# Cross attention in a two-attention kernel: wider weight loads for the transposes of P, and the projections moved between their two halves

## The chip, the cores and the metric

The kernel runs on one core of a Trainium2 chip. The metric is the device time of one execution in microseconds (us), as the median of several runs. Engines are named as in the profile: PE is TensorE's matmul, PEld its weight load, DVE VectorE, ACT ScalarE, POOL GpSimd, SP SyncE.

## The reference, cut to what matters

A batch of 32 sequences of 128 tokens, width 128, goes through a cross attention, a mixture of experts, a second cross attention (16 heads of width 8 over 77 context tokens) and two layers of local attention with a feed-forward part. The change touches only the second cross attention:

```python
def _L1_xattn_ref(q, k, v, mask, w_q, w_k, w_v, w_o):
    ...
    query = proj(q, w_q)
    key_ = proj(k, w_k)
    value = proj(v, w_v)
    scores = jnp.einsum('bhqd,bhkd->bhqk', query, key_) / jnp.sqrt(jnp.asarray(D_K, dtype=query.dtype))
    scores = jnp.where(mask == 0, jnp.asarray(NEG, dtype=scores.dtype), scores)
    attn = jax.nn.softmax(scores, axis=-1)
    out = jnp.einsum('bhqk,bhkd->bhqd', attn, value)
    out = out.transpose(0, 2, 1, 3).reshape(B, -1, H * D_K)
    return out @ w_o.T
...
x = x + _L1_xattn_ref(_layernorm(x, axis=-1), ctx_1024, ctx_1024, mask_1x1xSxS2_ik0, L1_xattn_w_q, L1_xattn_w_k, L1_xattn_w_v, L1_xattn_w_o)
```

## The kernel before, in words

The stages follow one another: first attention (tiles `a_...`), routing and experts (`r_...`, `b_...`), second cross attention (`c_...`), local attention (`d_...`) and feed-forward (`f_...`). The second cross attention is a software pipeline over the 32 sequences. Each engine runs its own program, written out by hand (`c_tensor`, `c_scalar`, `c_vector`, `c_pool`), once per step; `it.b(5)` is the sequence that is five steps old, and semaphores are all that ties the engines. In one step, in this order:

- PE: the transposes of the probabilities P of the older sequence, heads 0 to 7 (L1311, eight transposes of `c_p` into `slot1`; I call them PTa), then mask and scores of the next sequence, heads 0 to 7 (L1321, L1326; Sa), then heads 8 to 15 of both (PTb, Sb, the same lines), then the three projections of a yet younger sequence (L1337 values, L1338 queries, L1339 keys), then P times V (L1353), the transpose of the normalised input (L1360) and the output projection (L1364).
- ACT: copies PTa out of PSUM (L1378 `c_pT`), exponentials of heads 0 to 7 (L728, eight activations), copies PTb out, copies the projections out (L1387 to L1391), exponentials of heads 8 to 15.
- DVE: reciprocal of the sums of heads 8 to 15 (L1415 `c_rc`), layer norm, the largest score of each head after Sa and after Sb (L1407 `c_nm`), the mix of the experts' answers into X (L1436) and its statistics (L1440 to L1445), reciprocal of heads 0 to 7 (L1415), splitting of the projections into high and low parts (L1452 to L1461), copies and the sum into X (L1473 to L1478).
- POOL: normalises P of heads 8 to 15 (L1510 `c_p`), gathers expert answers (L1523, L1527), a reciprocal root (L1031 `rs`), the copy of a context (L1539 `c_c`), normalises P of heads 0 to 7 (L1510).

Every engine works its list off in order. PTa waits for the last of POOL's entries in the step before it, and PTb for the first of its own step. Both halves of the transposes use the two banks of `slot1`, so PTb also waits until ACT has copied PTa out. `c_p` holds, for each of 128 tokens, 16 rows of 77 probabilities, one head behind the other. In a few of the steps large copies for a later stage (`wqkv`, `w1l`) stand behind the step's own work on ACT and DVE.

Of the kernel before, what the change touches and what calls it, by code (L numbers as in the profile page):

```python
# [16 lines left out]
NB = 32  # L17
T = 128
D = 128
SK = 77  # L20
# [82 lines left out]
def nth(n, j, k):  # L103

    return (n - 1) * k + j


def count(b, j=1, k=1, base=0):

    return (b + base) * k + j  # L110


def program(nc, out, x_in, ctx_in, mask_in, wq0_in, wkv0_in, wo0_in, nrm0_in, wg_in, w1e_in, w3e_in, w2e_in,
            l1_in, wqkv_in, qks_in, wol_in, lng_in, w1l_in, b1l_in, w2l_in,
            ident_in, band_in, rot_in, keyi_in, head_in):
    with ExitStack() as ctx:
        def sem(name):
            return ctx.enter_context(nc.semaphore(name))
# [5 lines left out]
        def at(name, shape, dt=F32):  # L124
            size = 2 if dt == BF16 else 4
            for n in shape[1:]:
                size *= n
            t = nc.alloc_sbuf_tensor_at(name, shape, dt, offset=room[0])
            room[0] += (size + 31) // 32 * 32
            assert room[0] <= nc.sbuf_usable_end, name  # L130
            return t


        R = [ctx.enter_context(nc.psum_tensor(f"slot{i}", [128, 2, 512], F32)) for i in range(4)]
# [10 lines left out]
        ident = at("ident", [128, 128])  # L145
# [81 lines left out]
        l1 = at("l1", [128, 4, 128])  # L227
# [106 lines left out]
        def S(name):  # L334
            if name not in made:
                made[name] = sem(name)
            return made[name]
# [950 lines left out]
        def c_tensor(e):  # L1288
            t = c_

            def body(it):
                if it.static and it.i == 2:
                    e.wait_ge(S("b_xl"), LAST + 1)
                    e.wait_ge(S("c_const"), 1)
                if it.static and it.i == 4:
                    e.wait_ge(S("b_gT"), LAST + 1)
                    e.wait_ge(S("b_ye"), LAST + 1)
                if it.static and it.i == 5:
                    e.wait_ge(S("b_g"), LAST + 1)
                for half, slot in ((0, 2), (1, 3)):  # L1300
                    b = it.b(5)
                    if b is not None:
                        if half == 0:
                            if it.seen(6):
                                e.wait_ge(S("ac_pTb"), it.upto(6, NB))
                        else:
                            if it.seen(5):
                                e.wait_ge(S("ac_pTa"), it.upto(5, NB))
                        e.wait_ge(S("c_pn"), count(b, half + 1, 2))
                        for k in range(8):  # L1310
                            mm = e.transpose(R[1][0:SK, k // 4, 128 * (k % 4):128 * (k % 4) + 128],  # L1311
                                             t["p"][:, it.m(5, 2), 8 * half + k, :], ident[:])
                        mm.then_inc(S(("ac_PTa", "ac_PTb")[half]), 1)
                    b = it.b(4)
                    if b is not None:
                        e.wait_ge(S("c_sp"), count(b, 1, 3))
                        e.wait_ge(S("c_sp"), count(b, 3, 3))
                        if it.seen(5):
                            e.wait_ge(S("c_rc"), nth(it.upto(5), half + 1, 2))
                        for k in range(2):  # L1320
                            e.matmul(R[slot][:, k, 0:4 * SK], identb[:], maskb[:].rearrange("p a b -> p (a b)"),  # L1321
                                     start=True, stop=False)
                        for n, (w, x) in enumerate(((1, 0), (0, 1), (0, 0))):
                            for k in range(2):
                                o = 32 * (2 * half + k)
                                mm = e.matmul(R[slot][:, k, 0:4 * SK], t["qT"][w][o:o + 32, it.m(4, 2), :],  # L1326
                                              t["kb"][x][o:o + 32, it.m(4, 2), :, :].rearrange("p a b -> p (a b)"),
                                              start=False, stop=(n == 2))
                        mm.then_inc(S(("ac_Sa", "ac_Sb")[half]), 1)
                b = it.b(3)  # L1330
                if b is not None:
                    if it.seen(4):
                        e.wait_ge(S("c_sp"), nth(it.upto(4), 3, 3))
                    e.wait_ge(S("ac_xh"), count(b, base=NB))
                    e.wait_ge(S("ac_ch"), count(b, base=NB))
                    c = t["c"][:, it.m(3, 4), :]
                    e.matmul(R[0][0:SK, 0, 256:384], c, l1[:, 2, :], start=True, stop=True)  # L1337
                    e.matmul(R[0][:, 0, 0:128], l1[:, 0, :], t["xT"][:, it.m(3, 2), :], start=True, stop=True)  # L1338
                    e.matmul(R[0][:, 0, 128:128 + SK], l1[:, 1, :], c, start=True, stop=True).then_inc(S("c_proj"), 1)  # L1339
                if it.b(5) is not None or it.b(2) is not None or it.b(6) is not None:  # L1340
                    if it.seen(6):
                        e.wait_ge(S("ac_oTe"), it.upto(6, NB))
                    if it.seen(3):
                        e.wait_ge(S("ac_xh"), it.upto(3, NB))
                    if it.seen(7):
                        e.wait_ge(S("ac_add"), it.upto(7, NB))
                b = it.b(5)
                if b is not None:
                    e.wait_ge(S("ac_pTb"), count(b, base=NB))
                    for j in range(4):  # L1350
                        for g in range(4):

                            mm = e.matmul(R[0][32 * g:32 * g + 32, 1, 0:128],  # L1353
                                          t["vz"][0:SK, it.m(5, 4), g, 32 * j:32 * j + 32], t["pT"][0:SK, 4 * g + j, :],
                                          start=(j == 0), stop=(j == 3))
                    mm.then_inc(S("ac_PV"), 1)
                b = it.b(2)
                if b is not None:
                    e.wait_ge(S("ac_xn"), count(b, base=NB))
                    e.transpose(R[0][:, 1, 128:256], t["xn"][:, it.m(2, 2), :], ident[:]).then_inc(S("ac_xTp"), 1)  # L1360
                b = it.b(6)
                if b is not None:
                    e.wait_ge(S("ac_oTe"), count(b, base=NB))
                    e.matmul(R[0][:, 1, 256:384], t["oT"][:, it.m(6, 2), :], l1[:, 3, :], start=True, stop=True)\  # L1364
                        .then_inc(S("ac_wo"), 1)
            return body
# [786 lines left out]
```

## Time and profile before

| what | value |
|---|---|
| median of 3 runs | 1761.24 us (1760.27 to 1763.22) |
| the profiled execution | 1751.36 us |
| its span in the trace | 1749.4 us |
| busy: PE, PEld, DVE, ACT, POOL | 89%, 72%, 69%, 66%, 57% |
| the c stage, first transposes of P to the last | 624.1 to 992.0 us |

The profiled execution is 9.9 us shorter than the median, and 2.0 us of it lie outside the span. The page cuts the span into 40 slices of 43.7 us; the c stage lies in slices 15 to 23 counted from one. Busy shares are averages over stages with different limits, so the c stage has to be read by itself.

### The profile page before, as it was taken

Reading aid. Unit: us, or ns where it says so; the run is one execution under the profiler, and the core shown is the slowest. Engines: PE = TensorE matmul, PEld = TensorE weight load, DVE = VectorE, ACT = ScalarE, POOL = GpSimd, SP = SyncE. Lnnn points to the kernel's source line nnn. Section 1 sums busy time; section 2 is a strip of 40 time slices with the busy share of each in tenths; the row PEclk is TensorE's granted clock in tenths of the full one; section 3 lists DMA queues with packets and bytes.
Section 4 is the critical chain, followed back from the end, with each engine's and each line's share of the span. In section 5 each row is a group of like instructions: output and inputs, shape, how many; then the busy total and the mean of one; then the engine's idle time right before and its main releaser. Section 6 shows DMA issues by size and latency. Waiting matters only on the chain.

```text
span 1749.4 us, 37345 instructions
## 1 busy us (share of the span) xinstructions
PE 1555.5 (89%) x11418; PEld 1268.3 (72%) x11419; DVE 1210.9 (69%) x3059; ACT 1155.1 (66%) x3175; POOL 988.7 (57%) x853
## 2 busy tenths in 40 slices
PE   5899999899889879897877689999979799999988
PEld 3677777677667756665656478888868588888766
DVE  6888888888665554545555378888846677777656
ACT  5888788687555565666566467887753487777732
POOL 5668877688430055555554277777720577777500
PEclk8999999999999965557577699999999999999999
DMA  9700000000123210000000000000000000000000
GB/s 385 268 1 10 10 12 9 10 16 11 43 74 84 75 51 12 27 13 12 9 12 6 6 12 16 14 15 15 14 9 7 5 14 15 15 15 15 10 18 36
DMA packets 75555, 61.29 MB, mean 35 GB/s; under 512 B 40256, under 2 KB 61120, under 8 KB 74688
## 3 DMA queue, kind: packets, MB, share of 16 engines
q1 hardware_dynamic: 71360, 51.69, 9.2%
q0 software_dynamic: 4096, 8.40, 1.6%
q8 instruction: 47, 0.77, 0.2%
q14 instruction: 52, 0.43, 0.1%
HBM read 21.30 MB, written 30.41 MB: 30 GB/s over the span
## 4 chain that ended last, share of the span: by engine, by line
PE 57%; DVE 23%; ACT 6%; POOL 6%; issue 6%; DMA 1%; DVEq 0%; POOLq 0%; SPq 0%; ACTq 0%
PE slot L1311 6%; PE slot L1647 6%; PE slot L453 5%; PE slot L455 4%; PE slot L454 4%; PE slot L1630 4%; PE slot L1591 4%; PE slot L1326 3%; PE slot L1600 3%; ACT a_p L728 3%; PE slot L1665 3%; DVE a_sum L846 3%; POOL a_rq L1092 2%; PE slot L1881 2%; POOL c_p L1510 2%
## 5 line engine op out<-in xcount | busy, mean ns | idle before, releaser
L1031 POOL TENSOR_TENSOR rs<-mv,nhalf 128x1 f32 (+1 forms) x160 | 93.5, 584 | 276.9 <-DVE mv L1445 155.3
L1797 POOL TENSOR_TENSOR d_A<-d_A,d_B 128x1024 f32<-128x1024 f32 x64 | 150.7, 2355 | 130.2 <-DVE d_B L1743 130.2
L1801 POOL TENSOR_TENSOR d_r<-d_vv,nhalf 128x16 f32<-128x16 f32 x64 | 186.5, 2914 | 47.6 <-DVE d_vv L1765 47.1
L728 ACT ACTIVATE d_p<-slot,d_nm,d_r 128x128 f32<-128x128 f32 x512 | 186.0, 469 | 25.7 <-DVE d_nm L1756 25.7
L728 ACT ACTIVATE a_p<-slot,a_nm,a_rq 128x77 f32<-128x77 f32 x512 | 163.9, 433 | 54.8 <-DVE a_nm L754 54.8
L728 ACT ACTIVATE c_p<-slot,c_nm 128x77 f32<-128x77 f32 x512 | 143.8, 379 | 43.0 <-DVE c_nm L1407 43.0
L1311 PE MATMUL slot<-ident,c_p 128*77 128x128 f32 x512 | 113.0, 391 | 52.0 <-POOL c_p L1510 50.7
L1407 DVE TENSOR_REDUCE c_nm<-slot 128x8 f32<-128x616 f32 x64 | 51.1, 799 | 143.7 <-PE slot L1326 143.7
L1311 PEld LDWEIGHTS slot<-ident,c_p 128*77 128x77 f32 x512 | 92.0, 222 | 69.6 <-POOL c_p L1510 45.9
L1647 PE MATMUL slot<-d_v,d_pT 128*128 128x65 f32 x1024 | 121.8, 272 | 1.4 <-ACT d_pT L1684 1.4
L1378 ACT ACTIVATE c_pT<-slot 77x1024 f32<-77x1024 f32 x64 | 68.5, 1070 | 80.7 <-PE slot L1311 80.5
L1647 PEld LDWEIGHTS slot<-d_v,d_pT 128*128 128x128 f32 x1024 | 119.4, 192 | 2.1 <-ACT d_pT L1684 1.8
L736 POOL TENSOR_TENSOR a_p<-a_p,a_rc 128x616 f32<-128x616 f32 x64 | 80.1, 1251 | 72.1 <-DVE a_rc L848 71.7
L728 ACT ACTIVATION_READ_ACCUMULATOR c_p<-slot,c_nm 128x1 f32 x512 | 116.0, 230 | 0.0
L1724 DVE TENSOR_TENSOR d_A<-slot,T 128x1024 f32<-128x1024 f32 x64 | 78.3, 1224 | 44.4 <-PE slot L1591 42.9
L1752 DVE TENSOR_REDUCE slot<-slot 128x8 f32<-128x1024 f32 x64 | 78.9, 1233 | 31.4 <-PE slot L1630 28.6
L1092 POOL TENSOR_TENSOR a_rq<-a_vvq,nhalf 128x16 f32<-128x16 f32 x32 | 95.0, 2969 | 1.8 <-DVE a_vvq L961 1.8
L1695 ACT ACTIVATE d_oT<-slot 128x512 f32<-128x512 f32 x64 | 38.2, 597 | 78.3 <-PE slot L1641 78.3
L1510 POOL TENSOR_TENSOR c_p<-c_p,c_rc 128x616 f32<-128x616 f32 x64 | 78.8, 1232 | 18.4 <-DVE c_rc L1415 18.4
L607 PE MATMUL slot<-a_kb,a_qT 128*128 128x154 f32 x512 | 81.3, 303 | 8.4 <-DVE a_pT L889 7.3
L1527 POOL DMA_INDIRECT c_yg<-answers,c_gi x64 | 63.6, 994 | 36.7 <-POOL c_gi L1523 26.3
L1047 POOL DMA_INDIRECT routed<-r_xn,r_ps x64 | 65.0, 1016 | 34.1 <-issue 21.7
(282 smaller groups left out, 4738.9 us busy)
## 6 DMA issues: line engine op xcount, KB each, us to landing
routed<-zero SPq DMA_DIRECT2D x2, 9216.0 KB, 49.3
b_x<-routed SPq DMA_DIRECT2D x80, 64.0 KB, 1.8
answers<-b_y SPq DMA_DIRECT2D x40, 128.0 KB, 1.9
X<-in_x SPq DMA_DIRECT2D x2, 1024.0 KB, 7.3
d_zx<-Z SPq DMA_DIRECT2D x64, 32.0 KB
H<-Z SPq DMA_DIRECT2D x64, 32.0 KB
out<-f_o SPq DMA_DIRECT2D x8, 256.0 KB, 2.0
d_zx<-Z SPq DMA_DIRECT2D x64, 31.8 KB
```

The costliest lines, as they stand in the source:

```text
L453: e.matmul(o, ws[1], xs[0], start=True, stop=False)
L607: mm = e.matmul(R[slot][:, k // 2, 2 * SK * (k % 2):2 * SK * (k % 2) + 2 * SK], a["qT"][:, c, :], a["kb"][:, it.m(2, 2), c // 2, :], start ...
L728: i = e.activation(t["p"][:, h, :], R[slot][:, k // nbank, nk * (k % nbank):nk * (k % nbank) + nk], ACT.Exp, bias=t["nm"][:, h:h + 1], sca ...
L736: return e.tensor_tensor(p, p, t["rc"][:, h].unsqueeze(2).to_broadcast([128, h.stop - h.start, nk]), ALU.mult)
L1031: return e.tensor_tensor(rs[:, bass.ds(b, 1)], mv[:, bass.ds(b, 1), 1:2].rearrange("p a b -> p (a b)"), nhalf[:, 0:1], ALU.pow)
L1092: e.tensor_tensor(a["rq"][:, it.m(1, 2), :], a["vvq"][:], nhalf[:, 0:16], ALU.pow).then_inc(S("a_rq"), 1)
L1311: mm = e.transpose(R[1][0:SK, k // 4, 128 * (k % 4):128 * (k % 4) + 128], t["p"][:, it.m(5, 2), 8 * half + k, :], ident[:])
L1510: e.tensor_tensor(p, p, c_["rc"][:, h].unsqueeze(2).to_broadcast([128, 8, SK]), ALU.mult)\
L1647: mm = e.matmul(R[3][:, h // 4, 65 * (h % 4):65 * (h % 4) + 65], t["pT"][:, 4 * (h % 2) + h // 2, :], t["v1"][:, it.m(5, 4), h, :], start= ...
L1752: e.tensor_reduce(R[1][:, 0, 0:8], R[2][:].rearrange("p a (j k) -> p a j k", k=128), AX.X, ALU.max, negate=True)\
L1797: e.tensor_tensor(t["A"][:, p, :], t["A"][:, p, :], t["B"][:, p, :], ALU.add).then_inc(S("d_key"), 1)
L1801: e.tensor_tensor(t["r"][:, it.m(2, 4), :], t["vv"][:, p, :], nhalf[:, 0:16], ALU.pow).then_inc(S("d_key"), 1)
```

## The change

The transposes of P take their weights from `flat`, in which the eight heads of a half lie behind one another. Each now loads 128 columns instead of 77, from the start of its head, except the last of a half, which loads 77. Rows 77 to 127 of the transposed result hold columns of the next head, and no instruction reads them: the copy by ACT (L1378) and P times V take rows 0 to 76, as before. The block of the three projections moves from behind Sb to between Sa and PTb, with its waits. The other engines' programs are as they were.

```diff
                         e.wait_ge(S("c_pn"), count(b, half + 1, 2))
+                        flat = t["p"][:, it.m(5, 2), 8 * half:8 * half + 8, :].rearrange("p h k -> p (h k)")
                         for k in range(8):
-                            mm = e.transpose(R[1][0:SK, k // 4, 128 * (k % 4):128 * (k % 4) + 128],
-                                             t["p"][:, it.m(5, 2), 8 * half + k, :], ident[:])
+                            w = min(128, (8 - k) * SK)
+                            mm = e.transpose(R[1][0:w, k // 4, 128 * (k % 4):128 * (k % 4) + 128],
+                                             flat[:, SK * k:SK * k + w], ident[:])
                         mm.then_inc(S(("ac_PTa", "ac_PTb")[half]), 1)
...
                         mm.then_inc(S(("ac_Sa", "ac_Sb")[half]), 1)
-                b = it.b(3)
-                if b is not None:
-                    if it.seen(4):
-                        e.wait_ge(S("c_sp"), nth(it.upto(4), 3, 3))
-                    e.wait_ge(S("ac_xh"), count(b, base=NB))
-                    e.wait_ge(S("ac_ch"), count(b, base=NB))
-                    c = t["c"][:, it.m(3, 4), :]
-                    e.matmul(R[0][0:SK, 0, 256:384], c, l1[:, 2, :], start=True, stop=True)
-                    e.matmul(R[0][:, 0, 0:128], l1[:, 0, :], t["xT"][:, it.m(3, 2), :], start=True, stop=True)
-                    e.matmul(R[0][:, 0, 128:128 + SK], l1[:, 1, :], c, start=True, stop=True).then_inc(S("c_proj"), 1)
+                    if half == 0:
+                        b = it.b(3)
+                        if b is not None:
+                            if it.seen(4):
+                                e.wait_ge(S("c_sp"), nth(it.upto(4), 3, 3))
+                            e.wait_ge(S("ac_xh"), count(b, base=NB))
+                            e.wait_ge(S("ac_ch"), count(b, base=NB))
+                            c = t["c"][:, it.m(3, 4), :]
+                            e.matmul(R[0][0:SK, 0, 256:384], c, l1[:, 2, :], start=True, stop=True)
+                            e.matmul(R[0][:, 0, 0:128], l1[:, 0, :], t["xT"][:, it.m(3, 2), :], start=True, stop=True)
+                            e.matmul(R[0][:, 0, 128:128 + SK], l1[:, 1, :], c, start=True, stop=True).then_inc(S("c_proj"), 1)
```

On PE, one step of the c stage stands like this before the change; the names are tiles of the program, output before inputs, and the sizes are those of the output.

```order
L1311 MATMUL slot<-ident,c_p 77x128 x8
L1321 MATMUL slot<-maskb,identb 128x308 x2
L1326 MATMUL slot<-c_kbh,c_qTl 128x308 x2
L1326 MATMUL slot<-c_kbl,c_qTh 128x308 x2
L1326 MATMUL slot<-c_kbh,c_qTh 128x308 x2
L1337 MATMUL slot<-l_127,c_c 77x128
L1338 MATMUL slot<-c_xT,l_127 128x128
L1339 MATMUL slot<-c_c,l_127 128x77
L1353 MATMUL slot<-c_pT,c_vz 32x128 x16
```

These rows begin with PTb: the projections follow Sb and P times V follows them. After the change the same engine has, from PTa of a step on:

```order
L1313 MATMUL slot<-ident,c_p 128x128 x7
L1313 MATMUL slot<-ident,c_p 77x128
L1323 MATMUL slot<-maskb,identb 128x308 x2
L1328 MATMUL slot<-c_kbh,c_qTl 128x308 x2
L1328 MATMUL slot<-c_kbl,c_qTh 128x308 x2
L1328 MATMUL slot<-c_kbh,c_qTh 128x308 x2
L1340 MATMUL slot<-l_127,c_c 77x128
L1341 MATMUL slot<-c_xT,l_127 128x128
L1342 MATMUL slot<-c_c,l_127 128x77
L1313 MATMUL slot<-ident,c_p 128x128 x7
L1313 MATMUL slot<-ident,c_p 77x128
```

Seven of the eight transposes of a half write 128 rows instead of 77, and the three projections stand ahead of PTb and Sb instead of behind Sb. No instruction is added or removed.

## Rows read from the trace of the kernel before

**Rows 1.** The page: busy by engine, PE's granted clock in 40 slices.

```profile
span 1749.4 us, 37345 instructions
PE 1555.5 (89%) x11418; PEld 1268.3 (72%) x11419; DVE 1210.9 (69%) x3059; ACT 1155.1 (66%) x3175; POOL 988.7 (57%) x853
PEclk8999999999999965557577699999999999999999
```

**Rows 2.** Stretches: length, busy by engine, granted clock, DMA share, GB/s.

```profile
611.00:996.00 385.00, 312.74 (x2341) 238.16 (x2342) 189.95 (x633) 228.60 (x1191) 189.11 (x244) 0.63 0.06 17
648.20:736.90 88.70, 81.49 (x529) 61.89 (x527) 42.78 (x142) 52.25 (x274) 46.48 (x60) 0.50 0.07 20
736.90:743.70 6.80, 4.13 (x57) 3.24 (x57) 4.83 (x19) 4.23 (x27) 2.89 (x5) 1.00 0.04 10
```

**Rows 3.** Timeline of PE over one step at the lower clock, and the step's neighbours.

```profile
669.61 1.99 PE L1311 MATMUL slot<-ident,c_p 128*77 128x128 f32 x8 [0.92 <-POOL c_p L1510]
...
673.11 1.99 PE L1311 MATMUL slot<-ident,c_p 128*77 128x128 f32 x8
...
676.61 0.71 PE L1337 MATMUL slot<-l,c_c 128*77 128x128 f32 x2
...
678.01 1.94 PE L1353 MATMUL slot<-c_pT,c_vz 77*32 77x128 f32 x32
...
681.70 0.71 PE L1311 MATMUL slot<-ident,c_p 128*77 128x128 f32 x2 [0.92 <-POOL c_p L1510]
```

**Rows 4.** The chain that ended last, in the same step.

```profile
676.72 0.80 DVE c_nm L1407
677.52 0.27 DVE X L1436
678.98 0.17 DVE mv L1445
679.99 0.48 POOL c_c L1539
680.46 1.19 POOL c_p L1510
681.70 1.35 PE slot L1311 x5
```

**Rows 5.** Timeline of POOL: both normalisations of P, and the gather between.

```profile
671.27 1.21 POOL L1510 TENSOR_TENSOR c_p<-c_p,c_rc 128x616 f32<-128x616 f32 x1
674.77 0.96 POOL L1527 DMA_INDIRECT c_yg<-answers,c_gi  x1 [0.31 <-issue]
```

**Rows 6.** Timeline of PE: first transposes of the stage, and PTa thirty steps on.

```profile
624.12 1.96 PE L1311 MATMUL slot<-ident,c_p 128*77 128x128 f32 x8 [3.36 <-POOL c_p L1510]
970.04 1.91 PE L1311 MATMUL slot<-ident,c_p 128*77 128x128 f32 x8
```

**Rows 7.** Timeline of PE in steps with some full clock.

```profile
734.27 1.99 PE L1311 MATMUL slot<-ident,c_p 128*77 128x128 f32 x8
736.05 0.72 PE L1321 MATMUL slot<-maskb,identb 128*128 128x308 bf16 x2
790.13 1.10 PE L1311 MATMUL slot<-ident,c_p 128*77 128x128 f32 x8 [2.46 <-POOL c_p L1510]
792.45 1.99 PE L1311 MATMUL slot<-ident,c_p 128*77 128x128 f32 x8
795.51 0.44 PE L1337 MATMUL slot<-l,c_c 128*77 128x128 f32 x2
796.01 0.34 PE L1339 MATMUL slot<-c_c,l 128*128 128x77 f32 x2
```

**Rows 8.** Timeline of PE in the d stage: transposes with 128-column weights.

```profile
1277.81 1.91 PE L1600 MATMUL slot<-ident,d_p 128*128 128x128 f32 x8
1279.51 0.64 PE L1627 MATMUL slot<-bandb,identb 128*128 128x512 bf16 x2
```

**Rows 9.** Timeline of PE: a step with a large copy on DVE.

```profile
710.08 1.99 PE L1311 MATMUL slot<-ident,c_p 128*77 128x128 f32 x8 [0.65 <-POOL c_p L1510]
```

## The prediction

> **What bounds the kernel now.** I read the page first. PE is busy 89% of the span, and its granted clock is near full everywhere but in the c stage, where the slices fall to 5 to 7 tenths [rows 1]. The table of stretches gives the mean over 611 to 996 us as 0.63 [rows 2]. The clock has two levels, 0.50 (1.2 GHz) and 1.00 (2.4 GHz): 648.2 to 736.9 is all at 0.50, then comes a stretch of 6.8 us at 1.00, 736.9 to 743.7 [rows 2]. So full clock held in (0.63 - 0.50) / 0.50 = 26% of 385 us, about 100 us, or some 15 stretches of 6.8 us.
>
> Then I read one step at the lower clock. PTa starts at 669.61 and the next one at 681.70: 12.09 us [rows 3]. PE runs without a gap from PTa through Sa, PTb and Sb until the projections start at 676.61. The chain of waits leaves PE there: DVE takes the largest scores at 676.72, mixes X at 677.52, finishes the statistics at 678.98, POOL copies the context at 679.99 and normalises P of heads 0 to 7 from 680.46, and PTa follows [rows 4]. This is a loop of two parts:
> - the **PE part**, from PTa to the reduction after Sb, 676.72 - 669.61 = 7.1 us at the lower clock;
> - the **DVE and POOL part**, 681.70 - 676.72 = 5.0 us, which TensorE's clock does not touch.
>
> The projections, P times V, the input's transpose and the output projection run beside the second part. PE still idles 0.92 us there [rows 3]. The mean step over thirty steps is (970.04 - 624.12) / 30 = 11.53 us [rows 6], so the full stretches give back, net of the steps disturbed by large copies, 0.56 us a step.
>
> **The move of the projections.** They start at 676.61 and P times V at 678.01, which makes 1.40 us at the lower clock [rows 3]. At full clock they begin at 795.51 and the last begins at 796.01 and takes 0.34, so 0.84 us at most [rows 7]. Today DVE and POOL cover them. After the change they stand between Sa and PTb, inside the PE part, and queued behind them are PTb and Sb. DVE waits for Sb, and its mix, POOL's root, context copy and normalisation wait for DVE. Is there slack before PTb that could absorb them? At the lower clock, no: PTb starts at 673.11 without an idle mark, while POOL's normalisation of heads 8 to 15 ended at 671.27 + 1.21 = 672.48 [rows 3, 5]. So PE alone set it, and 1.40 us go onto the loop. The other end of the bound: with PTa at full clock, PTb starts 2.32 us after it [rows 7], against a normalisation that ends 672.48 - 669.61 = 2.87 us after PTa in the step at the lower clock [rows 3, 5]; if it ended as late in that step, up to half a microsecond could be absorbed. In the steps with a large copy there is slack too, 0.65 us [rows 9], in about three steps. The gather on POOL ends at 675.73 [rows 5], 3 us ahead of its next use, and is no bound. The sequences have projections ahead of PTb or Sb in 31 steps: 31 x 1.40 = **+43 us**. Off that go 3 x 0.65 = **-2 us**. What the move takes off PE's list behind Sb is worth nothing, since PE was not late there; it turns 0.92 us of idle into 2.3.
>
> **The wider loads.** Seven transposes of eight load 128 columns instead of 77. The first of eight 77-column transposes starts at 734.27 and the instruction behind them at 736.05: 1.78 us at the lower clock [rows 7]. Eight 128-column transposes in the d stage, also at the lower clock by the same division, take 1279.51 - 1277.81 = 1.70 us [rows 8]. The load width does not set the pace, and I cost the edit at **0**. The load lies beside the previous transpose; uncovered, it could cost at most a few hundredths of a microsecond per transpose. The Trainium skill speaks against this ("TensorE: Matmul & The Clock Gate", section LDWEIGHTS): a load takes its number of columns at 1.2 GHz, so 51 more columns would be some 43 ns, and if none of it were covered, 14 x 32 x 43 ns = 19 us, an estimate by that page. The two rows disagree with it as a cost on the path.
>
> **The clock.** This is the open term. PE work at full clock takes 1.10 us where it takes 1.99 at the lower one, or 0.44 against 0.71: a factor of 1.6 to 1.8, and I take 1.75 [rows 3, 7]. One full stretch of 6.8 us that spans the 5.0 us of DVE and POOL leaves 1.8 us for the PE part, which saves 1.8 x 0.75 = 1.35 us. The rise at 736.9 came just behind a burst of eight transposes, 734.27 to 736.05, in an unbroken run of PE since PTa [rows 7]. The step at 669.61 has the same run and no rise [rows 3], so the run as it is now is just enough in some steps and not in others. After the change the unbroken run is 8.5 instead of 7.1 us, and projections join directly onto a burst. I expect more stretches, 23 instead of 15 over thirty-odd steps: 8 x 1.35 = **-11 us**. In some five steps the projections themselves then run at full clock, saving 1.40 - 0.84 = 0.56 each: **-3 us**. The bounds: no rise at all would lose today's gift, 31 x 0.56 = 17 us, and full clock throughout the PE part would save far more (below). I take a value near the present state, since the content of the run hardly changes.
>
> The Trainium skill says of transposes on the same page (Part 4: PE-mode transpose) that they do not count as PE-busy in the way matmuls do. By that, only the moved projections would matter. The rise right behind eight transposes does not look like it.
>
> **Sum.** 43 - 2 - 11 - 3 = +27 us. On the profiled 1751.4 us this is 1778; the median is 9.9 us above the profiled execution, so 1761.2 + 27 = **1788 us**.
>
> **The rivals.**
> - *The clock pays for the move.* The longer run raises the clock early in nearly every step. At full clock the PE part would be about 8.5 / 1.75 = 4.9 us. Today's mean PE part is 11.53 - 5.0 = 6.5 us. The change gains once the new one is below that, when (8.5 - 6.5) / (8.5 - 4.9) = 56% of it runs at full clock. If a rise comes about 3 us into each step, the PE part is 3 + 5.5 / 1.75 = 6.1 us, and 31 x 0.4 less the 2 of the large copies makes -14 us: 1747. Full clock throughout would give 31 x 1.6 = -50 us: 1711. For it: today's run is at the edge of raising the clock. Against: in the stretch from 736.9 to 743.7, over DVE's and POOL's part, PE was busy for only 4.13 of 6.8 us, and then the clock fell [rows 2]; the change makes this idle time longer. Chance 0.28, of which 0.07 for far below 1740.
> - *The two cancel.* Rises in every step, but late in it: within 0.2%. Chance 0.07.
> - *Fewer rises.* PE's idle time of 0.92 us before PTa grows to 2.3, the busy share falls, and the clock stays low: 43 - 2 + 17 = +58, 1819 us. For it: the stage's clock is already the lowest of the kernel. Against: rises follow dense runs, and those get longer. Chance 0.08.
> - *Wider loads cost.* If the load sets the pace in part, some 10 to 19 us more: 1803. The d stage's rows speak against. Chance 0.05.
>
> **How the numbers follow.** The forecast has 0.52; its own range is 1776 to 1802: with no more stretches than today the sum is 43 - 2 - 0 - 0 = +41, with thirty it is 43 - 2 - 20 - 6 = +15. Slower than 0.2% (about what a measurement here can tell): 0.52 + 0.08 + 0.05 = 0.65; same 0.07; faster 0.28. The range for 8 in 10 takes in the first rival's moderate form and leaves out full clock throughout and most of the case without rises: 1742 to 1808.
>
> **What the changed profile would show.** At the lower clock PTa to PTb is 4.9 us instead of 3.5, and PTa to the reduction 8.5 instead of 7.1, with 5.0 behind it unchanged. Eight transposes take 1.8 us at the lower clock as before. PE's idle mark before PTa grows to about 2.3 us. The granted clock over the stage is 0.65 to 0.72. The a, b, d and f stages keep their times. I am wrong if the stage's clock is above 0.75, if the part behind the reduction is not 5.0 us, or if the eight transposes take over 2.0.

## The result and the profile after

The changed kernel takes 1806.92 us (median of 4 runs, 1800.59 to 1810.39), against 1760.76 us for the kernel before in the same comparison: ratio 1.026, 95% interval 1.0239 to 1.0281. It is 46 us slower. The forecast was 1788 us, 27 us slower, with a range of 1742 to 1808: the direction and the place were right, the size was short by 19 us. The result lies 1 us inside that range and above the 1776 to 1802 of the forecast's own mechanism.

The profiled execution took 1800.59 us. Of the page, the busy shares and PE's granted clock in 40 slices:

```profile
span 1798.6 us, 37345 instructions
PE 1565.9 (87%) x11418; PEld 1278.0 (71%) x11419; DVE 1216.0 (68%) x3059; ACT 1160.5 (65%) x3175; POOL 989.3 (55%) x853
PEclk9999999999989856655655679999999999999999
```

Against [rows 1] PE is busy 10.4 us more, DVE and ACT some 5 us, POOL 0.6 us, while the span grew by 49.2 us: most of the added time is waiting. The stretches of the c stage (length, busy by engine, granted clock, DMA share, GB/s):

```profile
631.00:985.00 354.00, 276.39 (x1969) 214.48 (x1969) 160.35 (x541) 195.13 (x1003) 166.28 (x214) 0.57 0.05 13
676.80:683.60 6.80, 3.33 (x51) 2.46 (x51) 4.84 (x19) 4.15 (x24) 2.20 (x4) 1.00 0.04 10
690.50:693.80 3.30, 1.62 (x37) 1.18 (x35) 2.75 (x10) 2.38 (x17) 0.39 (x1) 1.00 0.00 0
693.90:741.60 47.70, 38.97 (x248) 30.55 (x249) 21.44 (x72) 25.38 (x126) 25.05 (x32) 0.50 0.09 25
```

Over these 27 steps the clock is 0.57, so it is full for 14% of them; before it was 0.63 and 26% over the whole stage [rows 2]. In the full stretch from 676.80 PE is busy for 3.33 of 6.8 us; in the one of before in [rows 2] it was 4.13. For a fair comparison, the first 28 steps from PTa to PTa, of the kernel before and then of the changed one:

```profile
624.12:950.50 326.38, 275.29 (x2043) 210.00 (x2043) 167.58 (x561) 197.98 (x1040) 170.23 (x219) 0.62 0.05 14
631.02:998.37 367.35, 287.30 (x2043) 222.91 (x2043) 166.10 (x561) 202.22 (x1040) 170.29 (x219) 0.57 0.05 12
```

They take 41 us more. Over the first thirty steps (624.12 to 970.04 us before, 631.02 to 1016.85 us after) the trace of before has 13 stretches of full clock, 88 us in all; the changed one has 12, but seven of them are only half as long, and they make 63 us.

One step at the lower clock, timeline of PE:

```profile
695.66 1.97 PE L1313 MATMUL slot<-ident,c_p 128*128 128x128 f32 x8 [3.53 <-POOL c_p L1513]
697.42 0.72 PE L1323 MATMUL slot<-maskb,identb 128*128 128x308 bf16 x2
...
699.14 0.71 PE L1340 MATMUL slot<-l,c_c 128*77 128x128 f32 x2
...
700.41 1.91 PE L1313 MATMUL slot<-ident,c_p 128*128 128x128 f32 x8
...
703.83 1.94 PE L1356 MATMUL slot<-c_pT,c_vz 77*32 77x128 f32 x32
...
708.92 0.69 PE L1313 MATMUL slot<-ident,c_p 128*128 128x128 f32 x2 [2.32 <-POOL c_p L1513]
```

It answers to [rows 3]. From PTa to the end of Sb, where the next block begins, it is 703.83 - 695.66 = 8.17 us; before it was 676.61 - 669.61 = 7.00. The step is 708.92 - 695.66 = 13.26 instead of 12.09 us. Both differences are 1.17 us. PE's idle mark before PTa went from 0.92 to 2.32. The eight transposes take 697.42 - 695.66 = 1.76 us, as they did with 77 columns.

Over thirty steps, and where the stage begins (timeline of PE):

```profile
617.63 0.68 PE L1340 MATMUL slot<-l,c_c 128*77 128x128 f32 x2 [1.31 <-POOL c_c L1542]
631.02 0.45 PE L1313 MATMUL slot<-ident,c_p 128*128 128x128 f32 x1 [4.58 <-POOL c_p L1513]
1016.85 0.85 PE L1313 MATMUL slot<-ident,c_p 128*128 128x128 f32 x6 [0.68 <-POOL c_p L1513]
```

The mean step is (1016.85 - 631.02) / 30 = 12.86 us, against 11.53 [rows 6]: 30 x 1.33 = 40 us. Of this, 1.17 a step is the longer step at the lower clock. The other 0.16 is a balance (13.26 - 12.86 = 0.40 us a step by which the mean is shorter, formerly 0.56): the full stretches give back less, and the steps with large copies cost less than before. The first projections of the stage start 5.8 us later than in the trace of before:

```profile
611.83 0.47 PE L1337 MATMUL slot<-l,c_c 128*77 128x128 f32 x1 [1.70 <-POOL c_c L1539]
```

That difference arose before any changed instruction, so it belongs to the two executions that were profiled, not to the change. 40 + 5.8 leaves 3 us: 1.17 for the one block of projections that runs ahead of an Sb before the first PTa, and 2 for the stage's end.

### The profile page after: what moved, and what is told of

It reads as the page before. It is cut to its first block, busy times and chain, and to the rows that moved or that the text cites. A ratio compares the mean times of both kernels' runs of the same rounds, so it can differ in the third digit from the quotient of the medians.

```text
span 1798.6 us, 37345 instructions
## 1 busy us (share of the span) xinstructions
PE 1565.9 (87%) x11418; PEld 1278.0 (71%) x11419; DVE 1216.0 (68%) x3059; ACT 1160.5 (65%) x3175; POOL 989.3 (55%) x853
## 4 chain that ended last, share of the span: by engine, by line
PE 58%; DVE 22%; POOL 6%; ACT 6%; issue 6%; DMA 1%; DVEq 0%; POOLq 0%; SPq 0%; ACTq 0%
PE slot L1313 6%; PE slot L1650 5%; PE slot L453 5%; PE slot L455 4%; PE slot L454 4%; PE slot L1633 4%; PE slot L1328 4%; PE slot L1594 4%; PE slot L1603 3%; ACT a_p L728 3%; PE slot L1668 3%; DVE a_sum L846 2%; POOL a_rq L1092 2%; PE slot L1884 2%; POOL c_p L1513 2%
## 5 line engine op out<-in xcount | busy, mean ns | idle before, releaser
L1313 PE MATMUL slot<-ident,c_p 128*128 128x128 f32 (+1 forms) x512 | 116.8, 403 | 88.9 <-POOL c_p L1513 87.8
L1313 PEld LDWEIGHTS slot<-ident,c_p 128*128 128x128 f32 (+1 forms) x512 | 100.5, 222 | 97.4 <-POOL c_p L1513 73.6
```

The costliest lines, as they stand in the source:

```text
L1313: mm = e.transpose(R[1][0:w, k // 4, 128 * (k % 4):128 * (k % 4) + 128], flat[:, SK * k:SK * k + w], ident[:])
```

## The experiments

Two theories of the change stood at first. **A**: the projections lie on the loop's PE part, the width of the loads is free, and most of the price comes from the lower clock. **B**: the width has a share, by its pace or by the clock. A second question came from the forecast's open term: what makes the clock fall in this stage, and what does it cost? The letters in an expectation are its own and go on from there. Ratios are against the kernel before, run beside each.

### e1: the wide loads alone

```diff
+                        flat = t["p"][:, it.m(5, 2), 8 * half:8 * half + 8, :].rearrange("p h k -> p (h k)")
                         for k in range(8):
+                            w = min(128, (8 - k) * SK)
-                            mm = e.transpose(R[1][0:SK, k // 4, 128 * (k % 4):128 * (k % 4) + 128],
-                                             t["p"][:, it.m(5, 2), 8 * half + k, :], ident[:])
+                            mm = e.transpose(R[1][0:w, k // 4, 128 * (k % 4):128 * (k % 4) + 128],
+                                             flat[:, SK * k:SK * k + w], ident[:])
```

> The kernel before with the 128-column loads alone. Theory A (the width is free and leaves the clock as it is): within 4 us of before, eight transposes 1.7 to 1.8 us at the lower clock, granted clock over the c stage 0.62 to 0.64. Rival B (wider loads keep the clock up): clock above 0.66 and 10 us or more faster. Rival C (wider loads cost): 10 to 19 us slower.

Measured: 1753.95 us, ratio 1.0004 (0.9993 to 1.0016). The stage in its trace, and one burst of transposes:

```profile
611.00:996.00 385.00, 318.98 (x2338) 242.69 (x2339) 189.13 (x632) 227.98 (x1189) 187.56 (x241) 0.61 0.06 16
```

```profile
672.30 1.97 PE L1313 MATMUL slot<-ident,c_p 128*128 128x128 f32 x8
674.06 0.72 PE L1323 MATMUL slot<-maskb,identb 128*128 128x308 bf16 x2
```

Eight wide transposes take 1.76 us and the clock is 0.61, just under what A named. The width does nothing that can be measured, either to the pace or to the clock. Rivals B and C fall, and with them the theory that the width has a share.

### e2: the move alone

The diff of the change without the lines of e1.

> The kernel before with the projections between Sa and PTb alone, loads of 77 columns. Theory A: PTa to the reduction after Sb is 8.3 us instead of 7.1 at the lower clock, the part behind it stays 5.0, and the time is that of the full change, 1800 to 1812. Rival: the full change owes part of its 46 us to the width, and this one lies at 1790 or below, or at 1820 or above.

Measured: 1796.87 us, ratio 1.0247 (1.0227 to 1.0268), which covers the change's 1.026. The time lies below A's 1800 and above the rival's 1790, because the kernel before took 1753.54 us beside this run and not 1760.76; the ratio decides. A step at the lower clock:

```profile
716.73 1.99 PE L1311 MATMUL slot<-ident,c_p 128*77 128x128 f32 x8 [2.31 <-POOL c_p L1511]
...
720.23 0.71 PE L1338 MATMUL slot<-l,c_c 128*77 128x128 f32 x2
...
721.50 1.91 PE L1311 MATMUL slot<-ident,c_p 128*77 128x128 f32 x8
...
724.92 1.94 PE L1354 MATMUL slot<-c_pT,c_vz 77*32 77x128 f32 x32
```

724.92 - 716.73 = 8.19 us, as in the change. Within these intervals the move is the whole effect.

### e3 and e4: idle transposes at the end of each step

```diff
                         .then_inc(S("ac_wo"), 1)
+                if it.b(5) is not None and it.b(0) is not None:
+                    for j in range(8):
+                        e.transpose(R[1][:, j // 4 % 2, 128 * (j % 4):128 * (j % 4) + 128], ident[:], ident[:])
```

They write slot1 after ACT has read it and before PTa overwrites it, and nobody reads the result. PE does more work, none of it useful. It stands in the first 27 of the 32 steps that have transposes of P. e4 has 16.

> The kernel before with eight transposes of the identity into slot1, which nobody reads, behind the output projection of each step of the c stage up to the 32nd. Theory D (the clock falls because PE's work thins out between Sb and the next PTa): the granted clock over the stage rises above 0.8 and the time falls by 20 to 60 us, to 1700 to 1740. Rival E (the clock does not follow this): eight transposes at the lower clock take 1.7 us against 0.9 us of idle time, so each step is 0.8 us longer and the time 1785.

> The same with sixteen. Theory D: clock at 0.95 or more over the stage, steps of 9.3 to 9.8 us, time 1695 to 1715, since sixteen transposes at full clock take 1.75 us against 2.3 us of idle time. Rival E: 2.5 us more per step, time near 1835.

Measured: e3 1706.12 us, ratio 0.9733 (0.9712 to 0.9755); e4 1709.27 us, ratio 0.9755 (0.9735 to 0.9775). Of e3's trace, the first 28 steps and one step of PE at full clock:

```profile
624.30:903.00 278.70, 220.00 (x2258) 177.17 (x2258) 166.36 (x560) 195.50 (x1040) 169.05 (x219) 0.91 0.06 16
```

```profile
672.94 1.10 PE L1311 MATMUL slot<-ident,c_p 128*77 128x128 f32 x8 [0.73 <-POOL c_p L1513]
...
675.25 1.10 PE L1311 MATMUL slot<-ident,c_p 128*77 128x128 f32 x8 [0.33 <-POOL c_p L1513]
...
677.17 0.44 PE L1337 MATMUL slot<-l,c_c 128*77 128x128 f32 x2
...
680.54 1.04 PE L1368 MATMUL slot<-ident 128*128 128x128 f32 x8
682.24 0.99 PE L1311 MATMUL slot<-ident,c_p 128*77 128x128 f32 x7 [0.66 <-POOL c_p L1513]
```

The granted clock is 0.91, against 0.62 over the same 28 steps before, and the step is 682.24 - 672.94 = 9.30 us instead of 12.09. PTa to the projections is 4.23 us instead of 7.00, and the rest stays 5.07. So theory D's forecast came, and rival E falls: more PE work between the output projection and the next PTa raises the clock, and the lower clock costs up to 2.8 us a step. That it has to stand in this gap, and that thin work there is what lets the clock fall, these two runs do not show.

Twice the filler brings nothing more in time, though it raises the clock over the same stretch from 0.91 to 0.95, as expected:

```profile
624.00:903.00 279.00, 232.72 (x2484) 191.95 (x2482) 167.35 (x565) 196.37 (x1041) 169.68 (x220) 0.95 0.06 16
```

The Trainium skill ("TensorE: Matmul & The Clock Gate", Part 4: PE-mode transpose) says that transposes do not count as PE-busy in the way matmuls do. Here filler made of nothing but transposes raised the granted clock from 0.62 to 0.91; the measurement decides against it.

### e5: the change with the same eight

> The changed kernel with the eight idle transposes at each step's end. Theory A (the move costs what stands on PE's part of the loop, and most of that price is the lower clock's): with the clock kept up the projections add 0.3 to 0.5 us a step, since PTb waits for POOL anyway until 2.3 us after PTa, so 1715 to 1725, against 1706 for the kernel before with the same filler. Rival F (the move costs the same 43 to 46 us whatever the clock): near 1750.

Measured: 1723.34 us, ratio 0.9814 (0.9787 to 0.9842). A step at full clock:

```profile
661.48 1.09 PE L1313 MATMUL slot<-ident,c_p 128*128 128x128 f32 x8 [2.53 <-POOL c_p L1516]
...
664.07 1.04 PE L1313 MATMUL slot<-ident,c_p 128*128 128x128 f32 x8
...
671.02 1.09 PE L1313 MATMUL slot<-ident,c_p 128*128 128x128 f32 x8 [0.88 <-POOL c_p L1516]
```

The step is 671.02 - 661.48 = 9.54, so the move costs 0.24 us here against 1.17 at the lower clock, and somewhat less than the 0.3 to 0.5 expected: PTb waits for POOL anyway in e3, idle mark 0.33, and the projections run in that time. The ratios of e5 and e3 differ by 0.0081, 14 us (8 to 20 by the two intervals), of which 31 x 0.24 = 7 is this. The clock over 27 steps is 0.88 instead of e3's 0.91:

```profile
623.40:906.00 282.60, 217.21 (x2185) 175.93 (x2186) 160.66 (x540) 189.41 (x1003) 166.76 (x214) 0.88 0.06 16
```

The other half is there in the first three steps, before the clock of e5 stays up (e5, then e3):

```profile
623.42 1.94 PE L1313 MATMUL slot<-ident,c_p 128*128 128x128 f32 x8 [4.59 <-POOL c_p L1516]
```

```profile
624.31 1.96 PE L1311 MATMUL slot<-ident,c_p 128*77 128x128 f32 x8 [3.37 <-POOL c_p L1513]
...
654.15 1.10 PE L1311 MATMUL slot<-ident,c_p 128*77 128x128 f32 x8 [0.62 <-POOL c_p L1513]
```

They take 661.48 - 623.42 = 38.06 us in e5 and 654.15 - 624.31 = 29.84 in e3, 8 us more. Rival F, 43 us at any clock, falls.

### e6: the projections between PTb and Sb

```diff
                         mm.then_inc(S(("ac_PTa", "ac_PTb")[half]), 1)
+                    if half == 1:
+                        ...
                     b = it.b(4)
```

The block of the projections stands there whole, and no longer behind Sb.

> The kernel before with the projections between PTb and Sb, loads of 77 columns. Theory A: they stand on the same part of the loop, so at the lower clock PTa to PTb is 3.5 and PTa to the reduction 8.2 to 8.5 us; time 40 to 50 us above before, as for the change. Rival G (the harm comes from tearing Sa and PTb apart, and with them ACT's copies): clearly less than 40.

Measured: 1792.28 us, ratio 1.0219 (1.0179 to 1.0259), 38 us slower, just under the 40 to 50 that A named; the interval, 31 to 45, holds the lower part of that. The step at the lower clock:

```profile
699.68 1.99 PE L1311 MATMUL slot<-ident,c_p 128*77 128x128 f32 x8 [3.52 <-POOL c_p L1511]
...
703.18 1.99 PE L1311 MATMUL slot<-ident,c_p 128*77 128x128 f32 x8
...
707.88 1.94 PE L1354 MATMUL slot<-c_pT,c_vz 77*32 77x128 f32 x32
```

PTa to PTb is back at 3.50, and PTa to the end of Sb is 8.20 all the same. Between these two places ahead of Sb it makes little difference. Rival G, that tearing Sa and PTb apart does the harm, has at most the few us by which 38 lies under e2's 43.

### e7: the projections at the head of the step

The same block ahead of the loop over the halves, before PTa's wait for POOL.

> The kernel before with the projections at the head of the step, ahead of PTa's wait for POOL. Theory A: they fill idle time there; the input's transpose is copied 0.4 us before PTa could start, so 1.0 us of 1.35 comes onto the loop at the lower clock, and PTa to the reduction stays 7.1. Time 1780 to 1790 if the clock stays at 0.63 over the stage; less if the shorter idle time raises it. Rival G: no cost, 1755.

Measured: 1745.16 us, ratio 0.993 (0.9907 to 0.9953): 12 us faster than before (8 to 16). Its first 28 steps, and a step whose clock is low at its start:

```profile
628.90:943.00 314.10, 241.65 (x2045) 191.70 (x2045) 167.87 (x564) 195.80 (x1040) 167.49 (x220) 0.72 0.05 14
```

```profile
785.83 1.84 PE L1321 MATMUL slot<-ident,c_p 128*77 128x128 f32 x8
787.51 0.43 PE L1331 MATMUL slot<-maskb,identb 128*128 128x308 bf16 x2
...
788.86 1.09 PE L1321 MATMUL slot<-ident,c_p 128*77 128x128 f32 x8 [0.30 <-ACT c_pT L1378]
...
792.79 1.08 PE L1353 MATMUL slot<-c_pT,c_vz 77*32 77x128 f32 x32 [1.96 <-ACT c_pT L1378]
...
794.96 0.71 PE L1307 MATMUL slot<-l,c_c 128*77 128x128 f32 x2 [0.60 <-DVE c_xT L1476]
...
796.23 1.91 PE L1321 MATMUL slot<-ident,c_p 128*77 128x128 f32 x8
```

Projections and PTa now form one burst, the clock rises behind PTa, and Sa, PTb and Sb run at 2.4 GHz. The step is 796.23 - 785.83 = 10.40 us. The clock is 0.72, against 0.62 over 28 steps before. The forecast of 1780 to 1790 was for an unchanged clock, and its price was too high besides. The next step is all at the lower clock:

```profile
796.23:808.65 12.42, 11.01 (x74) 8.57 (x74) 6.83 (x25) 6.85 (x37) 6.50 (x8) 0.50 0.04 12
```

It is 0.33 us longer than the 12.09 of before, not 1.0. At that price an unchanged clock would have given about 1766. The projections start behind DVE's copy of `c_xT`, as expected. In this step PE idles 12.42 - 11.01 = 1.41 us, more than the 0.92 of before; so the amount of idle time alone does not decide the level of the clock. Why this order raises it stays open.

### e8 and e9: how much filler, and e7 with filler

> The kernel before with twelve idle transposes. Theory D: between e3 and e4, which lie within 3 us of one another: 1700 to 1710, with fewer falls of the clock than eight and cheaper ones than sixteen.

Measured: 1708.43 us, ratio 0.9728 (0.9674 to 0.9781). The number between 8 and 16 makes no difference to the time that these runs can tell.

> The kernel of e7, projections at the head of the step, with the eight idle transposes at its end. Theory H (e7 gained through the clock alone, its position on the loop costs time): with the clock kept up by the filler nothing is left to gain, and the projections at full clock delay PTa by 0.2 to 0.4 us a step: 1710 to 1720, behind e3's 1706. Rival I (the position itself is better): below 1700.

Measured: 1737.27 us, ratio 0.9922 (0.9895 to 0.9949). Theory H's 1710 to 1720 and rival I's time below 1700 both missed: it is far behind e3, and no faster than e7 (0.993) beyond the intervals, although the filler raised the clock over the first 28 steps from 0.72 to 0.83. PE in one step:

```profile
789.82 0.31 PE L1336 MATMUL slot<-c_kbh,c_qTh 32*128 32x308 f32 x2
792.07 1.08 PE L1353 MATMUL slot<-c_pT,c_vz 77*32 77x128 f32 x32 [1.94 <-ACT c_pT L1381]
...
793.47 1.91 PE L1368 MATMUL slot<-ident 128*128 128x128 f32 x8
795.17 0.63 PE L1307 MATMUL slot<-l,c_c 128*77 128x128 f32 x2
...
796.37 1.29 PE L1321 MATMUL slot<-ident,c_p 128*77 128x128 f32 x8
```

With the projections gone from behind Sb, P times V waits 1.94 us for ACT's copy of PTb. Behind that hole the filler runs at the lower clock in this step, 1.70 us for eight, and the projections 1.20, and both stand ahead of PTa. So the filler seems to sit in the wrong gap here; a filler between Sb and P times V, which would test it, was not tried.

## Why the prediction was right or wrong

The result lies inside the range for 8 in 10, but close to its end, and above the 1776 to 1802 of the forecast's own mechanism: the range held because it was wide, not because the sum was good. The price of the move was right in kind; the clock term went the wrong way.

- **The loop and its two parts**: right. The part behind Sb kept its length, 708.92 - 703.83 = 5.09 us against 681.70 - 676.61 = 5.09, and the growth stands whole in PE's part. e6 shows it once more with another place in that part.
- **The move of the projections, +43 us**: the place right, the size somewhat high. The term took 1.40 us from [rows 3], which is the distance from the first projection to P times V. Measured is 1.17, so 31 x 1.17 = 36 us. In its new place the block takes 700.41 - 699.14 = 1.27, and PTb and Sb behind it take 703.83 - 700.41 = 3.42 instead of 676.61 - 673.11 = 3.50.
- **The wider loads, 0**: right, e1 at 1.0004. The rival in which they cost 10 to 19 us falls.
- **The large copies, -2**: right, as far as one trace tells. In the kernel before PTb waits for POOL in three such steps, 0.65 us in [rows 9]. After the change it has no idle mark in two of them, and in the third the wait shrinks from 2.24 to 1.47 us. In the same step as [rows 9] the copy is there, and PTb behind it starts at once:

```profile
722.43 1.76 DVE L1284 TENSOR_TENSOR wqkv0l<-stage,wqkv0h 128x1536 fp32r<-128x1536 f32 x1
```

```profile
726.93 1.91 PE L1313 MATMUL slot<-ident,c_p 128*128 128x128 f32 x8
```

- **The clock, -11 and -3**: wrong, and this is the step that failed. I expected more full stretches, 23 instead of 15, because the unbroken run of PE grew from 7.1 to 8.5 us. That run was misread. In [rows 3] neither the projections at 676.61 nor P times V at 678.01 has an idle mark, so PE's unbroken run was 12.09 - 0.92 = 11.17 us and already held the projections; after the change it is 13.26 - 2.32 = 10.94. The move lengthened the loop, and with it the idle time by 1.4 us, but not PE's run. Over thirty steps the full stretches went from 13 to 12 and from 88 to 63 us. They give back less: the 0.16 us a step of above, 5 us, and the 2 us that the large copies no longer cost, make +7 us instead of -14. The rival of fewer rises named the longer idle time, the mark going from 0.92 to 2.3, but priced only its end point of no rises at all, and had a chance of 0.08. That the idle time is what shortened the full stretches is argued: e3 and e5 fit it, while e7 idles more than before at the lower clock and still has the higher mean clock. Put together, 36 - 2 + 7 and 2 us at the stage's end make 43, as the two profiled executions differ in this and what follows, 49.2 - 5.8 = 43 us; the medians differ by 46, which is within the interval. So this term is 21 us off, the move's smaller size took 7 of them back, and the 2 us at the stage's end and 3 us between the profiled executions and the medians make up the 19 us of the miss.
- **The rival in which the clock pays**: it did not, in this order. e7 shows that with the same three projections at the head of the step, where they stand mostly in idle time, the clock rises to 0.72; e3 shows that a clock of 0.91 is worth 2.7%.
- **What the profile was to show**: 4.9 us from PTa to PTb (measured 4.75), 8.5 from PTa to the reduction (8.3), 5.0 behind it, 1.8 for eight transposes, idle mark 2.3 all came; the clock of 0.65 to 0.72 did not.

## What to carry to other kernels

In a loop that crosses engines, find out which part of each engine's list stands on the loop and which is covered; moving work from the covered part into the loop costs its length less the slack that it meets there (1.17 us of 1.27 here at the lower clock, 0.24 us at full clock, where the next burst waited anyway), even where nothing is added, and turns cover into idle time. Where TensorE's granted clock lies at the lower level in one stage, try useless work in its idle time: a handful of transposes there was worth 47 us here, more than any order of the useful work that was tried. Before reasoning from the length of a burst, follow the engine's run through all instructions without an idle mark, covered ones included. Where filler has to stand is not settled: with the projections gone from behind Sb the same filler at the same place gained nothing over e7 (e9).

## What the runs showed of the hardware that was not expected

- The clock can stay at 1.2 GHz over long stretches in which PE is busy most of the time: 81.49 of 88.7 us [rows 2], and 38.97 of 47.7 us after the change. A step of e3 that is wholly at 2.4 GHz, the one from 672.94, has PE busy for a smaller share, 7.18 of 9.30 us.
- Weight loads of 77 and of 128 columns give the same pace of fp32 transposes: eight in 1.76 to 1.78 us at the lower clock.
- Eight idle transposes of 128 x 128 in each step, about 1.0 us of PE time at full clock, moved the mean granted clock over the stage's first 28 steps from 0.62 to 0.91.
